# A vision-transformer tower on one core: attention in three column chunks, feed-forward in four equal ones, query and key blocks ahead of the values

## What is computed

```python
h = concat(cls, patches @ W_lin.T + b_lin) + pos        # (32, 37, 256)
h = h + attn0(layernorm(h))      # 16 heads of 64, causal
h = h + ffn0(layernorm(h))       # 256 -> 1024 -> 256, piecewise linear gelu, rounded to 2**-8
h = h + attn1(layernorm(h))      # 16 heads of 64, not causal, + bo
x = layernorm(h)                 # 8 experts, each 256 -> 1024 -> 256
logits = x @ gate_weight.T
gates = logits * (logits >= kth_smallest(logits, 4*256*6))
h = h + sum_e gates[e] * (gelu(x @ w1[e].T + b1[e]) @ w2[e].T + b2[e])
```

## Time and profile before

| | us |
|---|---|
| median of three runs | 947.96 |
| the profiled execution, its own time | 949.03 |
| its span, first to last instruction | 947.2 |
| embedding, to the first query/key block | 0 to 34.9 |
| attention 0, first scores to the first scores of unit 20 | 43.2 to 213.2 |
| units 20 and 21, feed-forward | 213.2 to 304.4 |
| attention 1, first scores to those of unit 20 | 312.9 to 481.7 |
| units 20 and 21, router, first expert block | 481.7 to 509.3 |
| experts | 509.3 to 947.2 |

### The profile page before, as it was taken

One profiled execution on the slowest core, in us unless ns is written; L12 is line 12 of the kernel. 1 busy time (PEld: TensorE's weight loads), 2 busy tenths in 40 slices (PEclk: granted clock), 3 DMA queues, 4 the chain that ended last, 5 costly groups with the idle time before them and its releaser, 6 DMA issues.

```text
span 947.2 us, 19121 instructions
## 1 busy us (share of the span) xinstructions
PE 920.6 (97%) x7073; PEld 855.2 (90%) x7073; DVE 593.2 (63%) x1860; ACT 558.2 (59%) x1571; POOL 154.7 (16%) x173
## 2 busy tenths in 40 slices
PE   8999999999999999999999999999999999999998
PEld 8977888888877878888879999999999999999998
DVE  4677585858999774777667787644364534554333
ACT  4676565747665764756554645665566646575452
POOL 0342121211000221222210000711011101111012
PEclk9999999999999999999999999999999999999999
DMA  9310000001100210000002012102020111100001
GB/s 333 134 46 1 2 1 2 1 2 46 45 1 1 90 46 1 2 1 2 2 7 85 1 45 71 65 2 90 1 90 1 46 45 46 46 1 1 2 13 39
DMA packets 8800, 34.43 MB, mean 36 GB/s; under 512 B 642, under 2 KB 5122, under 8 KB 5380
## 3 DMA queue, kind: packets, MB, share of 16 engines
q1 hardware_dynamic: 8708, 33.22, 9.8%
HBM read 32.00 MB, written 1.21 MB: 35 GB/s over the span
## 4 chain that ended last, share of the span: by engine, by line
PE 49%; issue 33%; DVE 8%; POOL 6%; ACT 2%; POOLq 0%; DVEq 0%; ACTq 0%
PE D L591 17%; PE O L591 11%; POOL h L372 4%; PE T L772 4%; PE S L761 4%; PE O L786 4%; PE S L591 3%; PE D L613 2%; PE O L707 2%; PE O L860 1%; DVE probsT L1346 1%; PE T L649 1%; POOL h L384 1%; PE T L636 1%; ACT work L1022 1%
## 5 line engine op out<-in xcount | busy, mean ns | idle before, releaser
L1600 DVE TENSOR_TENSOR hid<-work,hid 128x296 fp32r<-128x296 f32 x256 | 136.7, 561 | 176.1 <-ACT hid L1139 175.3
L591 PE MATMUL O<-hid,wslot 128*128 128x296 f32 (+2 forms) x1680 | 238.4, 300 | 0.0
L591 PEld LDWEIGHTS O<-hid,wslot 128*128 128x128 f32 x1680 | 231.2, 189 | 0.6
L591 PE MATMUL D<-xn,wslot 128*128 128x296 f32 (+2 forms) x1368 | 220.5, 306 | 0.0
L591 PEld LDWEIGHTS D<-xn,wslot 128*128 128x128 f32 x1368 | 197.1, 189 | 3.9 <-DVE wslot L1167 0.2
L1135 ACT ACTIVATE work<-D,prm 128x296 f32<-128x296 f32 x128 | 66.1, 517 | 166.1 <-PE D L591 165.7
L1030 ACT ACTIVATE probs<-probs,negmax 111x111 f32<-111x111 f32 (+1 forms) x352 | 130.3, 372 | 36.2 <-DVE negmax L1331 36.2
L570 POOL TENSOR_TENSOR probs<-probs,rsum 111x444 f32<-111x444 f32 (+1 forms) x88 | 81.0, 921 | 363.3 <-DVE rsum L1339 363.3
L591 PE MATMUL S<-xn,wslot 128*128 128x296 f32 (+2 forms) x864 | 133.6, 301 | 0.0
L591 PEld LDWEIGHTS S<-xn,wslot 128*128 128x128 f32 x864 | 122.9, 189 | 0.1
L1331 DVE CUSTOM_DVE_ANT_0 probs<-S,maska 111x111 f32<-111x111 f32 (+1 forms) x352 | 73.1, 263 | 58.3 <-PE S L761 58.2
(11 more groups left out here) (180 smaller groups left out, 1191.9 us busy)
## 6 DMA issues: line engine op xcount, KB each, us to landing
raw<-in_moe SPq DMA_DIRECT2D x16, 1024.0 KB, 4.8
raw<-in_attn SPq DMA_DIRECT2D x7, 1024.0 KB, 4.9
work<-in_x SPq DMA_DIRECT2D x2, 1008.0 KB, 8.3
out<-h SPq DMA_DIRECT2D x4, 296.0 KB, 2.6
w2f<-in_attn SPq DMA_DIRECT2D x1, 1024.0 KB, 13.3
raw<-in_ffn SPq DMA_DIRECT2D x1, 1024.0 KB, 4.7
w2f<-in_ffn SPq DMA_DIRECT2D x1, 1024.0 KB, 4.8
raw<-in_x SPq DMA_DIRECT2D x2, 504.0 KB, 5.1
```

The costliest lines, as they stand in the source:

```text
L591: mm = pe.matmul(psum, a, b, start=(first and k == 0), stop=(k == 3 * n - 1))
L1600: nc.vector.tensor_tensor(moe_hid(s, 1), moe_g(s)[:, 0:w], moe_hid(s, 0).bitcast(F32), ALU.subtract).then_inc(m_hid, 1)
```

## The change

It cuts attention into three chunks of four, four and three groups (448, 448 and 298 columns), the feed-forward into four of 298, 298, 300 and 298, and leaves the embedding at four chunks (336, 336, 336, 186) and the experts at four of 296. `covering` finds how many chunks of one cut another cut's columns need. The halves now have 4, 4, 4, 4, 3, 3 units. In the last unit of a half that has blocks, all blocks stand ahead of `values` (`values_last`), and DVE takes `low_out` of that step one step later. `ffs` is gone: a third of the feed-forward buffers lie in columns 300 to 449 of `work`, in four runs of half a block; `logT` and `b1row` lie in `w2f`, so the load of the bias row waits for the value weight's split, and the load of the second feed-forward weight for the bias. `hid` has three slots of half a chunk. The norm of chunk 0 moves back: its mean after `embed(1, 1)`, its variance after `embed(2, 1)`; `variance(2, 0)` moves behind `ff_down(2, 1)`. Layer norm, router and logits go by three chunks.

```diff
-GC = 3
+GC = 4
 CW = GC * GW
 NC = -(-NG // GC)
+EG = 3
+EW = EG * GW
+EC = -(-NG // EG)
+ECHUNKS = [(c * EW, min(EW, T - c * EW)) for c in range(EC)]
+FC = 4
+FCUT = [0, 298, 596, 896, T]
+FCHUNKS = [(FCUT[c], FCUT[c + 1] - FCUT[c]) for c in range(FC)]
+MC = 4
...
+def covering(cuts, end):
+    return next(i for i, (a, w) in enumerate(cuts) if a + w >= end) + 1
...
+HALVES = 3
+WW = FW + FW // 2
...
-        hid = sb("hid", [P, 2, 2, KH * CW], F32R)
-        work = sb("work", [P, HEADS, CW])
-        ffs = sb("ffs", [P, 6, CW])
+        hid = sb("hid", [P, HALVES * 2 * QH * CW], F32R)
+        work = sb("work", [P, HEADS, WW])
...
+        def normed_from(n, c):
+            end = sum(CHUNKS[c])
+            return (KD * covering(ECHUNKS, end), KD * (c + 1), KD * covering(FCHUNKS, end), KD * (c + 1))[n]
...
             if p % 3 == 0:
-                three = [ffs[:, 2 * k:2 * k + 2, :] for k in range(3)]
+                three = [work[:, 4 * k:4 * k + 4, FW:WW].rearrange("p (i h) n -> p i h n", i=2) for k in range(3)]
...
+        def values_last(u):
+            p, n = place_in_half(u) if u < NUNIT else (0, 0)
+            return p == n - 1 and len(qk_blocks(u)) > 0 and out_due(u) is None
+
+        def blocks_first(u):
+            if out_due(u) is not None:
+                return 0
+            return len(qk_blocks(u)) if values_last(u) else 1
...
                 if i == W2_FF:
                     sp.wait_ge(*piece_split(V_ATTN0))
+                    sp.dma_start(b1row[0:1, :], b1_in).then_inc(b1_landed, 16)
+                    sp.dma_start(b1row[BL:BL + 1, :], b1_in).then_inc(b1_landed, 16)
+                    sp.wait_ge(b1_ready, 3)
                     sp.dma_start(w2f[:, :], weights[i - FIRST_W]).then_inc(w2_in, 16)
...
(PE, attention)
-                        for i in blocks[:1]:
+                        for i in blocks[:blocks_first(u)]:
                             project_qk(i)
                     if 0 <= u - 1 < NUNIT:
                         values(u - 1)
...
                         router(1)
-                        mean(3, 3)
-                        router(2)
-                    for i in blocks[0 if due is not None else 1:]:
+                        mean(3, NC - 1)
+                    for i in blocks[blocks_first(u):]:
                         project_qk(i)
...
(PE, start)
             embed(1, 0)
-            mean(0, 0)
             embed(1, 1)
-            variance(0, 0)
-            for c in (2, 3):
+            for c in range(2, EC):
+                if c == 2:
+                    mean(0, 0)
                 for dc in range(KD):
                     embed(c, dc)
+                    if (c, dc) == (2, 1):
+                        variance(0, 0)
             attention(0, 0)
...
(PE, feed-forward)
-                if (c, m) == (NC - 1, 3):
+                if (c, m) == (FC - 1, 5):
                     mean(2, 0)
+            ff_down(FC - 2, 1)
             variance(2, 0)
-            ff_down(NC - 2, 1)
             for dc in range(KD):
-                ff_down(NC - 1, dc)
+                ff_down(FC - 1, dc)
...
(DVE, start)
             set_h(1, 0)
+            set_h(1, 1)
             center(0, 0)
-            set_h(1, 1)
             low_part(4)
+            set_h(2, 0)
+            set_h(2, 1)
             root = newton(0, 0)
-            set_h(2, 0)
             apply(0, 0, root)
-            set_h(2, 1)
             low_part(FIRST_W)
...
(DVE, attention)
                     if u < NUNIT:
                         row_max(2 * u + 1)
+                    if u >= 1 and values_last(u - 1):
+                        low_out(u - 2)
...
-                    if 0 <= u - 1 < NUNIT:
+                    if 0 <= u - 1 < NUNIT and not values_last(u):
                         low_out(u - 1)
...
(DVE, feed-forward)
-                if p in (10, 14):
-                    ff_out1(p // 4 - 2, 1)
-                if p == 3 * KH // 2:
+                if p in (10, 13):
+                    ff_out1((p - 10) // 3, 1)
+                if p == NP - 1:
                     center(2, 0)
-            root = newton(2, 0)
-            ff_out1(NC - 2, 1)
-            apply(2, 0, root)
+            ff_out1(FC - 2, 1)
+            finish(2, 0)
```

More of the change, by code:

```diff
@@ L409, in moe_gate @@
         def moe_gate(e, c):
-            return work[:, 8 + (e % 2) * NC + c, :]
+            return work[:, 8 + (e % 2) * MC + c, :]
         def heads_out(k, c, half, a, nt):
-            m = QH * half
-            return hid[:, c % 2, k, :].rearrange("p (m n) -> p m n", n=CW)[:, m:m + QH, a:a + nt]
+            at = (2 * ((2 * c + half) % HALVES) + k) * QH * CW
+            return hid[:, at:at + QH * CW].rearrange("p (m n) -> p m n", n=CW)[:, :, a:a + nt]
         def out_pair(nt):
@@ L882, in _ @@
                 if (c, m) == (1, 1):
-                    mean(1, 3)
+                    mean(1, NC - 1)
                 if (c, m) == (1, 4):
-                    variance(1, 3)
-                if c >= 1 and m == (5 if c == NC - 1 else 6):
+                    variance(1, NC - 1)
+                if c >= 1 and m == (5 if c == FC - 1 else 6):
                     ff_down(c - 1, 0)
@@ L921, in moe_up @@
                     if s == 0:
[L922 to L923 removed]
+                        variance(3, NC - 1)
+                    if s in (2, 3):
                         turn_logits(s - 2)
                     if s == 5:
[L926 removed]
+                        router(2)
                     if s == 6:
[L928 removed]
+                        turn_logits(2)
                     if spread_at(e, c, m) is not None:
                         spread_gate(spread_at(e, c, m))
[L931 removed]
+                    n = e * MC + c
                     if m % 2 and 1 <= n <= 5:
@@ L966, in moe_down @@
                         sum_counts(8 * j + 4 + 2 * dc)
-            steps = [(e, c) for e in range(E) for c in range(NC)]
+            steps = [(e, c) for e in range(E) for c in range(MC)]
             for n, (e, c) in enumerate(steps):
@@ L1053, in attention @@
                         exps(2 * u + 1)
-                    n = 0 if due is not None else 1
+                    n = blocks_first(u)
                     for i in blocks[:n]:
@@ L1112, in _ @@
             attention(1)
-            square(3, 3)
-            inv_root(3, 3)
+            square(3, NC - 1)
+            inv_root(3, NC - 1)
             def spread(i):
@@ L1621, in moe_out1 @@
                     moe_gate(e, c)[:, 0:w], ALU.add, ALU.mult).then_inc(m_y, 1)
-            finish(3, 3)
+            finish(3, NC - 1)
             for k in (SPLITS - 2, SPLITS - 1):
                 low_quarter(FIRST_W + W_MOE + 1, k)
-            steps = [(e, c) for e in range(E) for c in range(NC)]
-            for s in range(E * NC * KH):
+            steps = [(e, c) for e in range(E) for c in range(MC)]
+            for s in range(E * MC * KH):
                 n, m = s // KH, s % KH
-                if n >= NC and n + NC < E * NC:
+                if n >= MC and n + MC < E * MC:
                     e, c = steps[n]
@@ L1657, in _ @@
                     gate_low()
-                if m == 1 and n >= NC + 2:
+                if m == 1 and n >= MC + 2:
                     moe_out(*steps[s // KH - 2])
```

172 lines of the change are left out of this document (86 added, 86 removed).

## The result

| | before | after |
|---|---|---|
| median of four runs, us | 948.03 | 976.50 |
| lowest and highest | 947.93, 948.47 | 975.72, 976.77 |
| the profiled execution, own time and span | 949.03, 947.2 | 975.72, 973.9 |
| mean granted clock of TensorE | 0.999 | 0.979 |

The ratio of after to before is 1.0297 (95% interval 1.0285 to 1.0309): 28.5 us slower. The forecast was 954.4 us with a range from 945 to 961. The direction was right, the size was not, and the range did not hold the time.

A forecast was written before the change was run, and what follows sets the result against it. PE's work and waits were taken to bound attention, DVE and PE nearly together the feed-forward. Terms 9.25-15.8+6.2+4.9+2.4-14.2+6.2+7.4 summed to +6.4 us on 949.03, 955.4, less 1.07 for the median: 954.4, range 945 to 961.

The forecast's parts named there:

- The clock: Behind PE's new idle at the start and both last units, matmuls run at 1.2 GHz: some 5 us, 959.5; chance 0.10.
- The price of a matmul and of a step: Attention: 0.46 ns a column, 549 ns for 577, 8.1 us saved in all; a step with two 448-column blocks takes 6.92.
- the three waits of the norm steps in layer 0: Attention 0, second transposes: PE waits for DVE's newton, low_out and apply, 5.3 us in sum.
- unit 3's in layer 1: Attention 1, second transposes: PE waits 3.1 us for DVE's norm work and weight quarters.
- nineteen steps: First scores to the last half's first: 154.2 us in attention 0, 154.6 in attention 1; -15.8 and -14.2.
- The waits of the scores: Ends of halves in attention: 14 of 16 waits for ACT's block move go, saving 7.5 us.
- The start's wait: Ahead of attention 0, PE idles 5.2 us for the norm and first weight's split; first scores come 9.25 later.
- The feed-forward's +7.3: Last unit of attention 0 through feed-forward, +4.9 us, and attention 1's first eight blocks, +2.4.
- The last half: Each attention's last half has three units instead of two, without blocks: two steps of 5.4 and 6.0, +6.2 us per layer.
- The transposes don't wait: Attention's second transposes: DVE's chain fits, so 11.8 us of new wait go, 942.5 us; chance 0.16.
- The start is covered: Start of attention 0: the weight's split and apply hide, so 6.7 us go, 947.7 us; chance 0.08.
- The loss of DVE's fast form: Feed-forward: odd 149-column runs cost 48 one-source instructions 0.31 us more each, 15 us less some idle, 966; chance 0.04.

The follow-up runs named there:

- the repaired kernel: The changed kernel with newton and apply a step later, first query weight split ahead of the norm's newton, dummy matmuls in remaining waits: 945.98 us.
- the first experiment: The kernel before with only the new order, all blocks ahead of values in a half's last unit: 949.59 us, ratio 0.9988.
- one more condition: The kernel before with all blocks ahead of values only where the next half's blocks are 336 columns wide: 944.77 us, ratio 0.9962.

## Why the prediction was wrong

**The clock was the step that failed.** The sum priced every matmul behind the new waits at the full clock, so the clock stood in it at nothing; it cost about 18.0 us, and with it alone the time leaves the range. The prediction had it as a rival: "If the grant falls to 1.2 GHz there, matmuls behind each last twice as long for a while; no row shows the lower level, so I bound it between nothing and as long as the idle, some 5 us in all: 959.5. 0.10." Three things in it were wrong. The places: it named three waits, at the start and in both last units, and the fall also came behind waits of 1.75 to 2.93 us at four second transposes, all four of which it had itself priced at 1.9 to 3.1. These four lost 7.9. The price: "some 5 us in all" had no row behind it, and the three places that it named lost 10.1 (2.5, 3.4 and 4.2, each less than its own idle of 4.85, 4.16 and 4.94). The chance: the argument for 0.10 was a clock of 1.00 beside waits of up to 1.18 us, which says nothing of waits of 2 to 5 (the longest in the kernel before is 1.57, in the embedding). The Trainium skill, "TensorE: Matmul & The Clock Gate" (Part 1: The HAM clock gate), was quoted as speaking for this rival, an idle array falling to half its clock; the trace agrees, with 0.50 behind the waits of 4.16 to 4.94 us, and the rule should have moved the chance.

**The other terms**, by the table of stages. The price of a matmul and of a step held: the three waits of the norm steps in layer 0 were forecast as 1.9, 0.65 and 2.7 and are 1.75, 0.66 and 2.54; unit 3's in layer 1 as 3.1 and is 2.93; nineteen steps as 154.2 and 154.6 and are 155.0 and 154.3 without the clock's part. The waits of the scores are down to two, as forecast. The start's wait was forecast as 5.2 and is 4.85; that stage came out 1.45 lower, partly because the embedding's first matmuls were 1.2 us earlier in this execution (a wait ends at 16.3 us instead of 17.4). That is no effect of the change: the 56 dummy matmuls ahead of the embedding take 7.9 to 9.5 us over the traces of all kernels here, 9.3 in before's and 8.2 in after's. The feed-forward's +7.3 is +7.4, and DVE kept its fast form: 464 ns for 596 columns with one source against 776 with two, where the earlier trace rows have 502 and 850 for 672.

**The last half** is the other term that was mis-sized, twice by 2.1 us. It had three units as 5.4 and 6.0 us; they are 5.43 and 8.10. In the second, PE waits 1.38 us at values and 0.49 for the squares. The chain of waits shows why:

```profile
218.77 1.90 ACT wslot L1027
220.68 0.79 ACT probs L1075 x5
```

ACT splits a weight for 1.90 us ahead of the unit's last exponentials; DVE's reciprocal waits for them, and behind it stands the copy that values need. The step has no blocks to cover this. The prediction had costed ACT at nothing there. Another wait that was not forecast, 1.37 us in unit 5 of attention 0, is for DVE, which has just split the feed-forward's bias (L1334 and L1337, 2.6 us). It brought no fall.

**The rivals.** "The transposes don't wait" was not what happened, but it was the right thing to look at: taking `apply` out of their way brings 25.3 us. "The start is covered" was wrong by its 4.85 us of wait. The loss of DVE's fast form did not occur.

What stays open is why the same wait of 1.75 us is followed by a fall in one kernel and by none in two others, and one of 1.68 us by none. Two more waits of the changed kernel, each without a fall there, have one in other traces. The wait of 1.87 us for the squares at the feed-forward's end is followed by a stretch of 3.4 us with the first split earlier (first row) and with the dummies in all waits; the pair of 1.37 and 0.49 us in unit 20 of attention 1 is so in the repaired kernel (second row) and two others:

```profile
295.58 3.20 PE L699 MATMUL T<-sq,mean_w 128*128 128x448 f32 x4 [1.87 <-ACT sq L1049]
...
477.97 1.72 PE L695 MATMUL T<-sq,mean_w 128*128 128x444 f32 x2 [0.49 <-DVE sq L1255]
```

In the changed kernel these groups take 1.77 and 1.01 us. Executions of one kernel differ in this too (944.2 against 949.5 to 950.4 in the first experiment). I have only the rows for that and no run that settles it.

## What to carry to other kernels

Where a change makes PE wait longer than any wait of the kernel before did (1.57 us here), price the clock as well as the wait: here it cost 18.0 us, twice what everything else came to (+8.7), and a clock of 1.00 beside shorter waits was no evidence against it. The cure is to move the late work behind the copy that PE waits for (25.3 us here); dummy matmuls in the wait bring back only the clock (15.8). A larger chunk saves at each step edge, and costs time where a whole chunk has to be ready with nothing behind it: the start, the last units, the seam between two stages.

## What the runs showed of the hardware

- The granted clock fell to 0.50 behind PE waits of 1.75, 2.5, 2.9, 4.2 and 4.9 us in the changed kernel and of 1.62, 1.87, 2.17, 2.66, 3.90 and 5.91 in others, and behind two short waits close together (0.96 and 0.53 us with 1.3 us of work between them; 1.37 and 0.49). All 20 waits of 2 us or more in the profiled runs have a fall in them or behind them; waits of 1.68, 1.75 and 1.87 us and the pair of 1.37 and 0.49 stayed without one in some. The stretches lasted 3.4, 6.8 or 10.2 us, with PE busy for all of that time in some (236.60 and 461.10 above), so PE's being busy again does not restore the clock at once.
- A stretch of 3.4 us cost 1.55 us in an otherwise equal step (8.67 against 10.22), and twelve matmuls of 448 columns took 4.83 us in one and 2.61 to 2.70 outside.
- Small plain matmuls without a use, 128 by 128, kept the clock up: with them in the waits one stretch of 3.4 us was left of seven stretches, and 15.8 us came back.
- Where a fall comes in some executions only, the time of one program has two values (5 to 6 us apart in the first experiment, some 3 to 5 in the change without its wide chunks), and the granted clock of each run tells which one it is. A median lies on either by chance; the first experiment's ratio, with an interval around 1, hid a gain of 4 us that showed in all four runs with one more condition.
